# Selective scan: the inflow products leave VectorE, and ScalarE makes them transposed

## The reference, cut to what matters

```python
dt = jax.nn.softplus(jnp.einsum('bsd,ed->bse', x, dt_w) + dt_b)
A = -jnp.exp(log_A)
b = jnp.einsum('bsd,nd->bsn', x, B_w) + B_b
c = jnp.einsum('bsd,nd->bsn', x, C_w) + C_b
def step(h, inp):
    x_t, dt_t, b_t, c_t = inp
    A_bar = jnp.exp(A[None] * dt_t[..., None])
    h = A_bar * h + (dt_t * x_t)[..., None] * b_t[:, None, :]
    y = jnp.einsum('bdn,bn->bd', h, c_t) + D_skip * x_t
    return (h, y)
```

## Time and profile before

| what | us |
|---|---|
| median of 3 runs | 1011.29 |
| lowest and highest of them | 1003.93, 1012.12 |
| the profiled execution, its own time | 1012.23 |
| span of its trace | 1010.4 |

### The profile page before, as it was taken

The page is one execution under the profiler, slowest core; times in us unless marked ns, Lnnn a source line. Parts: engine busy times, 40 slices in busy tenths (PEclk is TensorE's granted clock), DMA queues, the critical chain, the costliest instruction groups (busy, mean ns, idle before and its releaser), DMA issues. The chain is left out here.

```text
span 1010.4 us, 12056 instructions
## 1 busy us (share of the span) xinstructions
PE 836.5 (83%) x3703; PEld 373.6 (37%) x3703; DVE 849.3 (84%) x793; ACT 588.2 (58%) x913; POOL 273.9 (27%) x147
## 2 busy tenths in 40 slices
PE   4589999999999999984464657777777579999998
PEld 3212212222222222233434223222223457888886
DVE  6688868878888988958988799999999755888876
ACT  2306757777777777772135443444443267888885
POOL 3700000000000000000100377998999600231110
PEclk9858979999999999997697688999999678999999
DMA  8412321211212110012002043444443011322111
GB/s 182 122 51 61 92 59 33 68 59 37 76 34 84 35 32 22 12 35 66 0 6 83 26 141 109 166 166 166 167 180 131 1 38 55 104 78 63 62 63 42
DMA packets 41515, 75.93 MB, mean 75 GB/s; under 512 B 7560, under 2 KB 25456, under 8 KB 40432
## 3 DMA queue, kind: packets, MB, share of 16 engines
q1 hardware_dynamic: 41464, 75.30, 23.5%
HBM read 64.99 MB, written 8.85 MB: 73 GB/s over the span
## 5 line engine op out<-in xcount | busy, mean ns | idle before, releaser
L788 ACT ACTIVATE prob<-ps 128x512 f32<-128x512 f32 x512 | 264.8, 605 | 115.3 <-PE ps L1409 112.7
L1034 DVE TENSOR_REDUCE nmax_k<-ps 128x2 f32<-128x1024 f32 x224 | 262.6, 1220 | 45.5 <-PE ps L1380 44.2
L1409 PE MATMUL ps<-qs,ks 96*128 96x512 bf16 x512 | 165.6, 396 | 8.6 <-ACT prob L788 3.9
L706 POOL TENSOR_TENSOR hc<-hst,cbr 128x1024 f32<-128x1024 f32 x64 | 152.5, 2407 | 10.2 <-DVE hst L1163 7.4
L1163 DVE TENSOR_TENSOR_SCAN hst<-ps,dbx 128x1024 f32<-128x1024 f32 x64 | 144.9, 2281 | 0.3
L1430 PE MATMUL ps<-prob,vq 128*16 128x512 f32 x1024 | 135.9, 608 | 0.8 <-ACT prob L788 0.7
L1591 PE MATMUL ps<-hc,ident 128*128 128x512 f32 x256 | 128.7, 627 | 8.7 <-POOL hc L706 7.6
L892 ACT ACTIVATE ps<-dt,a_neg 128x1024 f32<-128x1024 f32 x64 | 71.5, 1117 | 100.7 <-DVE hst L1163 100.7
L1252 DVE TENSOR_TENSOR act_l<-act_t,act_h 128x1024 fp32r<-128x1024 f32 x64 | 91.1, 1431 | 37.1 <-ACT act_h L961 37.1
L1409 PEld LDWEIGHTS ps<-qs,ks 96*128 96x128 bf16 x512 | 40.2, 97 | 169.3 <-ACT prob L788 108.2
L957 ACT ACTIVATE act_t<-ps,b_now 128x512 f32<-128x512 f32 x128 | 82.9, 683 | 25.5 <-PE ps L1641 25.5
(11 more groups left out here) (182 smaller groups left out, 1074.1 us busy)
## 6 DMA issues: line engine op xcount, KB each, us to landing
cbr<-s_dram SPq DMA_DIRECT2D x64, 512.0 KB, 3.7
gate<-c_dram SPq DMA_DIRECT2D x8, 1024.0 KB, 6.9
qs<-q_dram SPq DMA_DIRECT2D x16, 288.0 KB
ks<-k_dram SPq DMA_DIRECT2D x48, 96.0 KB
o_dram<-o_sb SPq DMA_DIRECT2D x16, 256.0 KB, 2.0
wf<-in_L_ffn_w SPq DMA_DIRECT2D x8, 256.0 KB, 3.0
wfq<-in_L_ffn_w SPq DMA_DIRECT2D x8, 256.0 KB, 3.0
km<-k_dram SPq DMA_DIRECT2D x56, 32.0 KB
```

The lines of the kernel that those rows point to most:

```text
L706: nc.gpsimd.tensor_tensor(hc[:, slot], hst[:, slot], cbr[:, slot], ALU.mult).then_inc(s_hc, 1)
L788: nc.scalar.activation(prob[:, n % 8], ps[:, 4 + (first + n) % 3], ACT.Exp, scale=ATT_SCALE).then_inc(s_exp, 1)
L1034: nc.vector.tensor_reduce(nmax_k[:, half, kk, 2 * pair:2 * pair + 2, qt], ps[:, 2 * pair:2 * pair + 2, :], AX.X, ALU.max, negate=True).the ...
L1409: nc.tensor.matmul(ps[:, 4 + (first + n) % 3], ks[p][:, kt // 4, j, kt % 4 * P:(kt % 4 + 1) * P], qs[p][:, half, j, :], start=True, stop=T ...
```

## The change

From state m = 6 on (`TURNED_FROM`), for the remaining 58 of 64 states, the inflow is made another way. `dtx` is transposed once for each sequence (`turn_dtx`, eight transposes of 128x128, then copied by ScalarE to `dtxt`), and so is B (`turn_b`, copied to `bt`). With time on the partitions B_n is one number for each partition. ScalarE (`scaled`) copies the eight 128x128 pieces of `dtxt` to `dtb`, each with a column of `bt` as its per-partition scale. TensorE (`fill`) transposes the eight pieces back into PSUM, and the scan reads its inflow there. For the first six states `fill` is the old pair of bfloat16 matmuls, and VectorE multiplies in place in PSUM.

`brow`, GpSimd's share of the products, and `dbx` are gone. The decay factors `abar` lie in SBUF now, in a ring of four; PSUM banks 0 and 1 and banks 2 and 3 take the inflows of even and odd states. `dtb` is double. The loops over groups of four states are written out. In the list of each engine some pieces of the second sequence's preparation stand at another place.

```diff
+TURNED_FROM = 6
...
-        dbx = sb("dbx", [P, RING, SEQ])
+        abar = sb("abar", [P, RING, SEQ])
         hst = sb("hst", [P, RING, SEQ])
         hc = sb("hc", [P, RING, SEQ])
-        brow = sb("brow", [P, SEQ])
...
+        dtb = sb("dtb", [P, 2, KT, D])
+        dtxt = sb("dtxt", [P, BATCH, KT, D])
+        bt = sb("bt", [P, BATCH, KT, NSTATE])
...
-        def abar(slot):
-            return ps[:, 2 + 2 * (slot % 2):4 + 2 * (slot % 2), :].rearrange("p k t -> p (k t)")
+        def inflow_ps(m):
+            return ps[:, 2 * (m % 2):2 * (m % 2) + 2, :]
+        def turned(m):
+            return m >= TURNED_FROM
+        def turned_before(m):
+            return sum(turned(j) for j in range(m))
+        Y_BANK = (4, 5, 2, 3)
...
-            def inflow_pool(b, k):
-                turn = ROUNDS * b + k
-                pool.wait_ge(s_brow, turn + 1)
-                if not (isinstance(turn, int) and turn < 1):
-                    pool.wait_ge(s_scan, RING * turn)
-                nc.gpsimd.tensor_tensor(dbx[:, RING - 1], dtx[:, b * SEQ:(b + 1) * SEQ], brow[:], ALU.mult).then_inc(s_dbp, 1)
             def outflows(b, k):
                 for n in range(RING):
                     outflow(b, RING * k + n, n, k)
-                    if n == 0:
-                        inflow_pool(b, k)
...
-            def factors(b, n, slot, turn):
-                m = NSTATE * b + n
-                if slot == RING - 1:
-                    act.wait_ge(s_bb, m + 1)
-                    if not (isinstance(m, int) and m < RING):
-                        act.wait_ge(s_dbp, turn)
-                    nc.scalar.activation(brow[:], ps[:, 0:2], ACT.Copy).then_inc(s_brow, 1)
-                if not isinstance(m, int):
-                    act.wait_ge(s_scan, m - 1)
-                elif m:
-                    act.wait_ge(s_scan, m if m < 3 else m - 1)
-                nc.scalar.activation(abar(factor_slot(m) if isinstance(m, int) else slot), dt[:, b * SEQ:(b + 1) * SEQ], ACT.Exp,
-                                     scale=a_neg[:, bass.ds(n, 1)]).then_inc(s_abar, 1)
+            def factors(m):
+                b, n = divmod(m, NSTATE)
+                if m >= RING:
+                    act.wait_ge(s_scan, m - RING + 1)
+                nc.scalar.activation(abar[:, m % RING], dt[:, b * SEQ:(b + 1) * SEQ], ACT.Exp,
+                                     scale=a_neg[:, n:n + 1]).then_inc(s_abar, 1)
+            def turned_dtx(b, half):
+                act.wait_ge(s_dxt_ps, 3 * b + half + 1)
+                nc.scalar.activation(dtxt[:, b, 4 * half:4 * half + 4].rearrange("p k c -> p (k c)"), ps[:, 4 + half],
+                                     ACT.Copy).then_inc(s_dxt, 1)
+            def turned_b(b):
+                act.wait_ge(s_dxt_ps, 3 * b + 3)
+                nc.scalar.activation(bt[:, b].rearrange("p k n -> p (k n)"), ps[:, 4, 0:KT * NSTATE],
+                                     ACT.Copy).then_inc(s_dxt, 1)
+            def scaled(m):
+                b, n = divmod(m, NSTATE)
+                t = turned_before(m)
+                act.wait_ge(s_dxt, 3 * (b + 1))
+                if t >= 2:
+                    act.wait_ge(s_tdb, t - 1)
+                for k in range(KT):
+                    ins = nc.scalar.activation(dtb[:, t % 2, k], dtxt[:, b, k], ACT.Copy, scale=bt[:, b, k, n:n + 1])
+                    if k % 4 == 3:
+                        ins.then_inc(s_dtb, 1)
...
-            factors(0, 0, 0, 0)
+            factors(0)
             norm_act(2, 1)
-            factors(0, 1, 1, 0)
+            factors(1)
             turn_act(2, 2, 5)
             turn_act(2, 3, 6)
             z_projected(2)
-            factors(0, 2, 2, 0)
+            factors(2)
             z_projected(3)
+            factors(3)
+            softplus_exp(1)
+            turned_dtx(0, 0)
+            turned_dtx(0, 1)
+            factors(4)
+            turned_b(0)
             act.wait_ge(s_bc, 2 * CHUNKS)
-            act.wait_ge(s_z, CHUNKS)
-            for n in range(3, PEEL):
-                factors(0, n, n % RING, n // RING)
-                if n in (3, 4, 6, 7):
-                    {3: softplus_exp, 4: first_parts, 6: softplus_ln, 7: second_parts}[n](1)
-            with act.Fori(PEEL // RING, NSTATE // RING) as k:
-                for n in range(RING):
-                    factors(0, RING * k + n, n, k)
-            act.wait_ge(s_dt, 3)
-            with act.Fori(0, NSTATE // RING) as k:
-                for n in range(RING):
-                    factors(1, RING * k + n, n, ROUNDS + k)
+            first_parts(1)
+            factors(5)
+            softplus_ln(1)
+            for m in range(TURNED_FROM, BATCH * NSTATE):
+                if turned(m):
+                    scaled(m)
+                if m == NSTATE:
+                    act.wait_ge(s_dt, 3)
+                factors(m)
+                if m == TURNED_FROM:
+                    second_parts(1)
+                if m == 20:
+                    turned_dtx(1, 0)
+                    turned_dtx(1, 1)
+                if m == 22:
+                    turned_b(1)
...
-            def inflow(b, n, slot):
-                if slot == RING - 1:
+            def inflow(m):
+                if turned(m):
                     return
-                m = NSTATE * b + n
-                dve.wait_ge(s_bb, m + 1)
-                if not (isinstance(m, int) and m < RING):
-                    dve.wait_ge(s_scan, m - RING + 1)
-                nc.vector.tensor_tensor(dbx[:, slot].rearrange("p (k t) -> p k t", k=2),
-                                        dtx[:, b * SEQ:(b + 1) * SEQ].rearrange("p (k t) -> p k t", k=2),
-                                        ps[:, 0:2], ALU.mult).then_inc(s_dbx, 1)
-            def scan(b, n, slot, turn):
-                m = NSTATE * b + n
-                if slot == RING - 1:
-                    dve.wait_ge(s_dbp, turn + 1)
+                b = m // NSTATE
+                dve.wait_ge(s_bb, m - turned_before(m) + 1)
+                nc.vector.tensor_tensor(inflow_ps(m), dtx[:, b * SEQ:(b + 1) * SEQ].rearrange("p (k t) -> p k t", k=2),
+                                        inflow_ps(m), ALU.mult).then_inc(s_dbx, 1)
+            def scan(m):
+                if turned(m):
+                    dve.wait_ge(s_tdb, turned_before(m) + 1)
                 else:
-                    dve.wait_ge(s_dbx, (RING - 1) * turn + slot + 1)
+                    dve.wait_ge(s_dbx, m - turned_before(m) + 1)
                 dve.wait_ge(s_abar, m + 1)
-                if not (isinstance(m, int) and m < RING):
+                if m >= RING:
                     dve.wait_ge(s_hc, m - RING + 1)
-                nc.vector.tensor_tensor_scan(hst[:, slot], abar(factor_slot(m) if isinstance(m, int) else slot), dbx[:, slot], 0.0, ALU.mult, ALU.add).then_inc(s_scan, 1)
+                nc.vector.tensor_tensor_scan(hst[:, m % RING], abar[:, m % RING], inflow_ps(m).rearrange("p k t -> p (k t)"),
+                                             0.0, ALU.mult, ALU.add).then_inc(s_scan, 1)
...
-            inflow(0, 0, 0)
+            inflow(0)
+            inflow(1)
             norm_dve_var(2, 1)
-            scan(0, 0, 0, 0)
+            scan(0)
             norm_dve_scale(2, 1)
-            inflow(0, 1, 1)
-            scan(0, 1, 1, 0)
-            inflow(0, 2, 2)
-            scan(0, 2, 2, 0)
+            scan(1)
+            inflow(2)
             bc_projected(2)
+            scan(2)
+            inflow(3)
             bc_projected(3)
-            for b in range(BATCH):
-                for n in range(0 if b else 3, PEEL):
-                    inflow(b, n + 1, (n + 1) % RING)
-                    scan(b, n, n % RING, ROUNDS * b + n // RING)
-                    if b and n == 1:
-                        skip(b - 1)
-                    if b == 0 and n in (4, 6, 7, 9):
-                        {4: softplus_u, 6: softplus_lost, 7: softplus_dt, 9: inflow_factor}[n](1)
-                dve.wait_ge(s_dt, 2 * BATCH)
-                with dve.Fori(PEEL // RING, NSTATE // RING - 1) as k:
-                    for n in range(RING):
-                        inflow(b, RING * k + n + 1, (n + 1) % RING)
-                        scan(b, RING * k + n, n, ROUNDS * b + k)
-                for n in range(NSTATE - RING, NSTATE):
-                    if NSTATE * b + n + 1 < BATCH * NSTATE:
-                        inflow(*divmod(NSTATE * b + n + 1, NSTATE), (n + 1) % RING)
-                    scan(b, n, n % RING, ROUNDS * b + n // RING)
+            scan(3)
+            inflow(4)
+            softplus_u(1)
+            scan(4)
+            inflow(5)
+            softplus_lost(1)
+            scan(5)
+            for m in range(TURNED_FROM, BATCH * NSTATE):
+                if m == NSTATE:
+                    dve.wait_ge(s_dt, 2 * BATCH)
+                inflow(m)
+                scan(m)
+                if m == TURNED_FROM + 1:
+                    softplus_dt(1)
+                if m == TURNED_FROM + 3:
```

(141 more changed lines are left out.)

## The result

The changed kernel takes 1021.32 us in the median of five runs (1018.36 to 1022.66); the kernel before took 1010.71 in five (1003.93 to 1012.12). The ratio is 1.0107, with a 95% interval of 1.0072 to 1.0142. The forecast was 1018.5 us with a range of 1000 to 1034. The profiled execution took 1021.32 us, its span is 1019.5, 9.1 more than before. The medians differ by 10.6 us, where the forecast had 7.2.

A forecast was written before the change was run, and what follows sets the result against it. VectorE was taken to bound the scan stage at 3.03 us a state, then ScalarE at 3.38; with start and end, skip(1) came 7.2 us later, 1019.4 profiled, less 0.94 for the median: 1018.5 us, range 1000 to 1034.

The forecast's parts named there:

- The bound: Steady scan stage: VectorE's 3.03 us a state gives way to ScalarE, whose beat becomes 3.38 us a state.
- The pitch of a small copy: ScalarE's 128x128 scaled copies, start to start: 0.29 us each, from 0.15 + 0.06 + 0.08, bounds 0.21 and 0.37.
- The bound of 0.21 for a copy without a pointer: Lower bound of the small copy's pitch on ScalarE, if the pointer's 0.08 us is hidden: 0.21 us.
- The bound for no overlap at all: Upper bound of the small copy's pitch, 0.37 us; as a rival, a 4.08 us beat and 1058 us, chance 0.06.
- TensorE: Steady scan stage: TensorE's work goes from 2.2 to 2.6 us a state, hidden below 3.38, with its clock staying.
- The rival in which it falls to half clock: Scan stage: TensorE waits four times a state and drops to half clock, beat 5.2 us, 1120 us; chance 0.03.
- The start: Start of the scan stage: ScalarE begins state 8 at 596 us, from a range of 594 to 597.4.
- the 576.2 of the sum: Start of the stage: estimated time when the last projection's B and C leave PSUM on VectorE, 574.70 before.
- The end: End of the stage: 6.9 us from the last exponential, at 786.8, to skip(1) at 793.7, before at 786.47.
- More overlap: Rival: small copies on ScalarE overlap more, pitch 0.21, giving 984 us; chance 0.12 for faster by over 1%.
- two of the stated cases: Chances for the whole kernel's time: within 1% of no change 0.52, slower by over 1% 0.36.
- break-even beat of 3.25 us: Scan stage: the beat per state at which the change neither wins nor loses, a small-copy pitch of 0.274 us.

The follow-up runs named there:

- lag_3: The changed kernel, but from state 44 on TensorE adds the outflow three states behind in place of four; 1017.71 us, ratio 1.0065 to the kernel before.

## Why the prediction was right

**The bound.** Right: VectorE's 3.03 us gave way to ScalarE's beat, forecast 3.38 and measured 3.37. **The pitch of a small copy**, the number on which the sign hung, was built from four neighbours at 0.29 and measured at 0.292; its pointer's share was taken at 0.08 and is 0.09. The bound of 0.21 for a copy without a pointer became 0.20 in the run that took it away. The bound for no overlap at all was put too low, at 0.37: one copy by itself is shown as 0.386. The Trainium skill, ScalarE: Activation LUTs, section "What ACT_TABLE_LOAD costs", has the figures for a small copy with a pointer, and the estimate worked out from them was 0.293. The trace agrees, with 0.292.

**TensorE.** Its load was forecast at 2.6 us a state, share 0.77, and its clock to stay. The clock stayed at 1.00. The work is 2.59; the share shown is 0.87, since a burst of four transposes counts 0.63 us busy and the pitch of one is 0.11, so tails overlap idle time. The forecast held its 0.77, which is work, against the 0.76 of the earlier trace rows, which is such a shown share; the two are not the same measure. The rival in which it falls to half clock didn't come.

**The start.** State 8 was forecast for 596 and came at 597.03. TensorE's chain began at 577.44, 1.2 us after the 576.2 of the sum, and ended at 582.97, within the 580.2 to 583.8. ScalarE's items took 14.03 us for 13.6. So the start came 1.0 us late in all.

**The end.** This is the term that was mis-sized. The sum had 6.9 us from the last exponential to `skip(1)`, with GpSimd's last product as the thing waited for. It took 796.07 - 787.77 = 8.30. The sum counted one total behind the last product, but five stood behind the last fill, 8.6 us of TensorE; `lag_3` showed 1.33 of the 1.4. Before, GpSimd's lag had hidden this backlog: TensorE waited for it ahead of the last total. 1.0 of the start and 1.4 of the end make the 2.4 by which 796.07 stands above 793.7.

**The rivals.** More overlap, which would have made it faster, needs a pitch under 0.274; the copies overlap by 0.09 and no more. The measured 1.07% stands on the border between two of the stated cases, 0.52 for within 1% and 0.36 for slower, and its interval covers both. That the forecast came within 3 us of the median is in part luck: the pitch was pieced together from rows of other code that are read to 0.01 us, 0.01 us of it is 4.5 us of time, and it came out right to 0.002. The start and the end both missed, to the same side. The 984 us of the rival with more overlap is 983 when it is counted from the median like the forecast. The break-even beat of 3.25 us explains why a change that moves so much work moves the time so little: VectorE and GpSimd gained 0.8 and 0.6 us a state, and ScalarE, the engine with the most room, was given 2.3, which put its beat, 3.38 us over the 56 states, 0.35 above the old one and 0.13 above the break-even. That is 7.2 us, and the 2.4 make it the 9.6 of the trace. With a third of the states left to VectorE the same code is 2.7% faster than the kernel before.

## What to carry to other kernels

Moving work off a full engine is worth what the fullest engine has afterwards, so write the beat of every engine for the share that is moved, and move the share at which two of them meet: 58 of 64 states lost 1.1%, two of three of them won 2.7%, every second one won 1.4%, none lost 2.1%, and no other share was run. Cost a row of small ScalarE instructions by their pitch among neighbours, here 0.09 us for each whatever its width, 0.09 more for a pointer and 0.85 ns a column, not by columns alone and not by the length shown. When an engine that was late is relieved, look at what its lateness hid, such as a backlog of another engine's queue at the stage's end.

## What the runs showed of the hardware

The 0.18 us that a small copy costs whatever its width, of which 0.09 are the pointer's, do not hide behind neighbours, even among eight equal independent ones (pitch 0.292 us with the pointer, 0.20 without, 0.40 at twice the width). VectorE and GpSimd can hold each other up. One operation of VectorE on two SBUF tiles took 3.25 us in the kernel before, where GpSimd was at its products:

```profile
578.31 9.73 POOL L706 TENSOR_TENSOR hc<-hst,cbr 128x1024 f32<-128x1024 f32 x4
...
585.88 3.25 DVE L1122 TENSOR_TENSOR bc<-bc,bcp 64x1024 f32<-64x1024 f32 x1
```

In the changed kernel the same operation took 1.22 us, with GpSimd idle from 581.96 to 588.15. Another one on two SBUF tiles took 3.26 there, with GpSimd's product beside it at 3.25 in place of 2.36:

```profile
584.36 1.22 DVE L1146 TENSOR_TENSOR bc<-bc,bcp 64x1024 f32<-64x1024 f32 x1 [1.85 <-ACT bcp L866]
...
599.58 3.25 POOL L716 TENSOR_TENSOR hc<-hst,cbr 128x1024 f32<-128x1024 f32 x1 [0.83 <-DVE hst L1184]
...
600.65 3.26 DVE L1157 SCALAR_TENSOR_TENSOR dt<-zt,dt 128x1024 f32<-128x1024 f32 x1
```

The scans, with one operand in PSUM, stayed at 2.28 us through the whole stage. It makes no difference to them which of the two operands lies there: their mean is 2281 ns before, with the decay factor in PSUM, and 2283 after, with the inflow in PSUM.
